# A third accumulator bank for the last part of a weight table, and two vector-engine steps in another order

## The reference, cut to what matters

```
x (32,32,512) f32
y0  = grouped_conv(x) + context + bias
out = oct_linear(silu(oct_linear(y0, Wgate)) * oct_linear(y0, Wup), Wdown)
x   = x + out                          # 1024 tokens of 512 values
y   = mix of 8 small kernels, by an attention net on cond_128, applied to x
x   = x + moe(y)                       # 32 experts, top 2, 512x512 each
```

## Time and profile before

| what | value |
|---|---|
| device time, median of 3 runs | 279.16 us (278.95 to 281.38) |
| the profiled execution: its own time | 279.04 us |
| its span, first to last instruction | 277.2 us |
| PE busy | 265.2 us, 96% of the span |
| DVE, ACT, POOL busy | 143.1, 77.8, 68.5 us |
| mean granted PE clock | 0.997 |

### The profile page before, as it was taken

How to read it: one execution, slowest core, us unless ns; L and a number is a source line. 1 busy time by engine, 2 the same in 40 slices (tenths; PEclk the granted TensorE clock), 3 DMA queues, 4 the chain that set the end, 5 groups by cost and what they waited for, 6 DMA issues and landing times.

```text
span 277.2 us, 4491 instructions
## 1 busy us (share of the span) xinstructions
PE 265.2 (96%) x1588; PEld 158.2 (57%) x1588; DVE 143.1 (52%) x423; ACT 77.8 (28%) x144; POOL 68.5 (25%) x67
## 2 busy tenths in 40 slices
PE   7888999999999999999999999999999999997991
PEld 3356677678866677878887665433333433332680
DVE  2577766766913342477541336520558521440885
ACT  1755564334212214233321121311011111113100
POOL 0711600000000000003705022453776352143200
PEclk9999999999999999999999999999999999999998
DMA  7999900000011100009905999962799999996937
GB/s 261 400 367 334 292 29 1 2 0 2 0 38 38 40 1 38 2 6 362 385 8 182 384 421 420 423 246 62 249 355 404 416 421 421 427 401 228 417 140 278
DMA packets 19590, 61.69 MB, mean 223 GB/s; under 512 B 4698, under 2 KB 6394, under 8 KB 15216
## 3 DMA queue, kind: packets, MB, share of 16 engines
q1 hardware_dynamic: 14816, 51.03, 47.7%
q0 software_dynamic: 3312, 7.80, 7.6%
q10 hardware_dynamic: 1440, 2.58, 2.5%
HBM read 54.39 MB, written 13.21 MB: 244 GB/s over the span
## 4 chain that ended last, share of the span: by engine, by line
PE 79%; DMA 8%; DVE 7%; issue 2%; SPq 1%; ACT 1%; DVEq 0%; ACTq 0%; POOLq 0%
PE bank L1452 29%; PE bank L1620 18%; PE bank L1655 15%; DMA wbuf<-r_tab 3%; PE bank L1507 3%; PE bank L1593 3%; DMA xp_first<-in_xp 3%; PE bank L1335 2%; DMA r_tab<-res,recs 2%; PE bank L1514 1%; PE bank L1345 1%; DVE acc L1308 1%; DVE acc L1303 1%; PE bank L1397 1%; PE bank L1564 1%
## 5 line engine op out<-in xcount | busy, mean ns | idle before, releaser
L1620 PE MATMUL bank<-wbuf,xT 128*32 128x512 f32 (+1 forms) x448 | 70.4, 597 | 1.8 <-DMA wbuf<-in_w 1.7
L1655 PE MATMUL bank<-md,hid 128*128 128x512 f32 x176 | 49.7, 418 | 0.0
L683 POOL DMA_INDIRECT slots<-kept,sid x16 | 15.9, 994 | 120.3 <-DVE sid L1072 117.3
L1620 PEld LDWEIGHTS bank<-wbuf,xT 128*32 128x32 f32 (+1 forms) x448 | 18.8, 119 | 37.6 <-issue 36.3
L1655 PEld LDWEIGHTS bank<-md,hid 128*128 128x128 f32 x176 | 31.3, 188 | 9.0 <-issue 4.1
L1452 PE MATMUL bank<-y0hi,mg 128*128 128x512 f32 x88 | 35.2, 412 | 0.2 <-ACT y0hi L758 0.2
L1452 PE MATMUL bank<-y0hi,mu 128*128 128x512 f32 x88 | 33.7, 396 | 0.7 <-DVE mu L958 0.7
L1452 PE MATMUL bank<-y0lo,mu 128*128 128x512 f32 x88 | 33.6, 393 | 0.0
L1452 PE MATMUL bank<-y0lo,mg 128*128 128x512 f32 x88 | 33.5, 392 | 0.0
L1109 DVE COPY xT<-bank 128x512 f32<-128x512 f32 x19 | 13.0, 690 | 37.6 <-PE bank L1593 36.0
L880 ACT ACTIVATE res<-bank,recs 128x512 f32<-128x512 f32 x19 | 13.1, 687 | 66.7 <-PE bank L1620 61.1
(11 more groups left out here) (208 smaller groups left out, 300.6 us busy)
## 6 DMA issues: line engine op xcount, KB each, us to landing
wbuf<-in_w SPq DMA_DIRECT2D x32, 1024.0 KB, 13.4
r_tab<-in_zero SPq DMA_DIRECT2D x1, 4096.0 KB, 25.8
wbuf<-r_tab SPq DMA_DIRECT2D x8, 512.0 KB, 7.3
acc<-in_x SPq DMA_DIRECT2D x1, 2048.0 KB, 15.2
y_tab<-yv SPq DMA_DIRECT2D x8, 256.0 KB, 5.1
out<-acc ACTq DMA_DIRECT2D x8, 256.0 KB, 2.4
base<-in_base SPq DMA_DIRECT2D x3, 352.0 KB, 7.2
xp_first<-in_xp SPq DMA_DIRECT2D x1, 1040.0 KB, 7.0
```

What stands on the lines that cost most here:

```text
L683: pool.indirect_dma_start(out=slots, out_offset=bass.IndirectOffsetOnAxis(ap=sid[:, j, k:k + 1], axis=0), in_=rec[:, j, k], in_offset=None ...
L1620: v = mm(RS[t % 2][p0:p0 + w], xT[x_slot(t)][:, c, p0:p0 + w], wbuf[buffer(r)][:, c], start=(c == 0), stop=(c == DC - 1))
L1655: v = mm(DN[j % 2][:], hid[:, t, part, c], md[:, c], start=(c == 0 and part == 0), stop=(c == HC - 1 and part == 1))
```

## The change

Up part 7 is made in bank 4 instead of bank 3. It waits for the first low half (`y0lo_done` at 1), the last reader of bank 4, in place of the copy of part 5, and it comes right behind part 5 on PE, ahead of part 6. The four gate products of chunk 1 are cut in two pairs with part 6 between them. `pu_mm` is counted in the new order. On DVE the copy of part 7 moves ahead of `conv_lo(1)`. In chunk 1 of the first half DVE does the copy of `up_rest(2)` first and `hid_lo(0)` behind it; all other chunks keep their order.

```diff
+UP_ORDER = (0, 1, 2, 3, 4, 5, 7, 6)
...
+        def up_bank(k):
+
+            return bank[4] if k == OCT - 1 else PU[k % 2]
...
             def up_table(k):
-                act.wait_ge(pu_mm, k + 1)
+                act.wait_ge(pu_mm, UP_ORDER.index(k) + 1)
...
             def up_table(k):
-                dve.wait_ge(pu_mm, k + 1)
-                nc.vector.tensor_copy(mu[:, :, 0:CUT, OB * k:OB * (k + 1)], in_bank(PU[k % 2], 0, CUT)).then_inc((pu_even, pu_odd)[k % 2], 1)
+                dve.wait_ge(pu_mm, UP_ORDER.index(k) + 1)
+                nc.vector.tensor_copy(mu[:, :, 0:CUT, OB * k:OB * (k + 1)], in_bank(up_bank(k), 0, CUT)).then_inc((pu_even, pu_odd)[k % 2], 1)
...
             conv_lo(0)
             up_table(5)
+            up_table(7)
             conv_lo(1)
-            up_table(7)
             conv_lo(2)
             conv_lo(3)
...
-                        if c >= 1:
+                        if c >= 2:
                             hid_lo(n - 1)
                         for kind, k in first:
                             if kind == "up":
                                 up_rest(k)
                             if kind == "down":
                                 down_high(k)
+                        if c == 1:
+                            hid_lo(n - 1)
                         hidden(n)
...
-                if k >= 2:
+                if 2 <= k < OCT - 1:
                     pe.wait_ge((pu_even, pu_odd)[k % 2], k // 2)
-                mm(in_bank(PU[k % 2], 0, CUT), perm[:, k], chunks(0, CUT)(tern[:, 1]), start=True, stop=True).then_inc(pu_mm, 1)
+                if k == OCT - 1:
+                    pe.wait_ge(y0lo_done, 1)
+                mm(in_bank(up_bank(k), 0, CUT), perm[:, k], chunks(0, CUT)(tern[:, 1]), start=True, stop=True).then_inc(pu_mm, 1)
...
-            def products(bank_, tab, n, half, parts):
-                for r in range(R):
+            def products(bank_, tab, n, half, parts, rs=range(R)):
+                for r in rs:
...
                 up_table(4)
                 up_table(5)
-                products(G[1], mg, 1, 0, (0,))
+                up_table(7)
+                products(G[1], mg, 1, 0, (0,), range(R // 2))
                 up_table(6)
-                up_table(7)
+                products(G[1], mg, 1, 0, (0,), range(R // 2, R))
                 pe.wait_ge(pu_even, OCT // 2)
                 pe.wait_ge(pu_odd, OCT // 2)
```

## The result

The changed kernel takes 278.09 us in the median of 10 runs (277.84 to 278.83), the kernel before 279.10 in 10 runs beside it (278.82 to 281.47). The ratio is 0.9956, with a 95% interval of 0.9936 to 0.9976; the two medians alone give 0.9964. The profiled execution after has a time of 278.11 and a span of 276.3, where before it was 279.04 and 277.2.

The account below looks back on a forecast made before the run. PE's order of work was taken to bound the kernel nearly everywhere. Gains of 0.48 and 0.32 make 0.80, so 279.04 - 0.80 = 278.24, stated as 278.3 given the runs' median, with a range of 277.7 to 279.3.

Parts of the forecast that it names:

- The first edit: PE, chunk 1: part 7 in bank 4 and part 6 between product pairs start the up products 0.48 us earlier.
- the hand-over: Copy to PE: 0.13 us from a copy's end to PE's start, used for every hand-over to PE.
- The second edit: DVE, chunk 1: up_rest(2) copied first opens PE's 0.69 stall; 0.32 comes through, 0.37 becomes a wait for POOL.
- rival (a): Down table: POOL is done in time or its hand-over is shorter, so all 1.17 comes, 277.9; chance 0.10.
- Rival (b): DVE and POOL: the moved low half meets POOL's L673, 0.80 shrinks to 0.11, 278.9; chance 0.07.
- To the end: From 32.5 to 245 us the chain stays on PE and the weight stream follows PE, so all 0.80 comes through.
- the wait for the last weights: Last stage: PE's 1.7 us wait before the last product, expected to stay near 1.7.
- Rival (c): Gain lost: up products no earlier, or weight stream doesn't follow PE and the last wait grows; 279.0, chance 0.14.
- Rival (d): Last stage: scatters or a load get ahead of the last weights on full DMA engines; 279.5, chance 0.11.

Follow-up runs that it names:

- e5: Changed kernel with the two waits ahead of the up products in the other order; one execution, 281.15 us, beside one of the kernel before of 281.61.
- e1: Only the part 7 and part 6 reordering, on the kernel before; DVE does hid_lo(0) first again in chunk 1; 282.98 us, ratio 0.9998.
- e6: e3 with part 6 in bank 7 and conv_lo(1) ahead of the copies of parts 5 and 7; one execution, 285.21 us, kernel before 281.61.
- e2: Only the DVE reordering in chunk 1 (copy of up_rest(2) ahead of hid_lo(0)), on the kernel before; ratio 0.9941.
- e3: Changed kernel with each part of the down table one place later on PE, ACT and DVE; 282.94 us, ratio 0.9962.
- e7: Kernel before with only the DVE reordering in chunk 1 and the down table one place later; one execution, 283.99 us, kernel before 281.61.
- r_before: The kernel before, unchanged, run and profiled once more on another chip than those with stops near 195 us; 279.13 us.

## Why the prediction was right

The forecast was 278.3 for a range of 277.7 to 279.3, and the median is 278.09. Against the profiled execution the sum said 0.80 less; that execution has 0.93 less, 1.12 when both are counted from the first gate product, and the medians differ by 1.01.

**The first edit.** Part 6 was forecast at 20.57 - 18.58 = 1.99 and came at 1.97, ACT's copy at 2.36 and came at 2.34, and ACT's copy is the last one. The up products were forecast at 3.03 and came at 2.88, the low products at 23.53 - 18.58 = 4.95 and came at 4.84. The term that was too large is the hand-over: I took 0.13 from the one row that had it and 0.05 for a start of the pipeline. Here it is 0.05 in all, and e5 shows that 0.1 of it goes with the order of the two waits. So the first edit is worth 0.63 at the up products, 0.59 at the low products and 0.57 further on (e1), instead of 0.48. I had the end of the first pair and the wait for the copy of part 4 as equal (20.56 and 20.57). In e6, without that wait, part 6 starts at the same place (1.98 against 1.97), so PE's own order is enough to set it.

**The second edit.** The stall of 0.69 opened up in full (0.14 between the rest parts), 0.31 of it came through, and 0.38 turned into the wait at L1407, where I had 0.32 and 0.37. e2 shows the same without the first edit, e3 and e7 show that 0.35 to 0.37 come back when the down table is asked for later. This was the step on which forecast and rival (a) differed, and POOL's three steps had the same lengths in every run, 2.05, 2.05 and 1.54, within 0.01.

**Rival (b)** asked that the low half hold POOL. It didn't: it ended at 28.66 + 0.73 = 29.39, POOL's last step started at 30.14, 0.09 behind the one before. What I had not seen is that the low half itself became short, 0.73 against 1.19 (below). It gave DVE 0.46 for which little came back: `hidden(1)` starts only at 29.61, after 0.21 of idle for which the profile names no one.

**To the end.** The 0.89 at 13.02 is 0.90 at conv 2, and at the first product of the last stage 0.97 (151.86 against 152.83). The end is 257.50 against 258.62, 1.12 less. The extra of about 0.2 lies in the last stage, and not in the wait for the last weights, which shrank from 1.7 to 1.0 where I had it near 1.7. The chain that ended last leaves PE for good at about 245 us, ten us before that wait ends: it goes on through an ACT copy, a scatter, SP and one load of the scattered rows, and then DVE to the end. In the kernel before (chain in order of time, 240 to 277 us):

```profile
245.18 0.70 ACT res L880
...
255.78 9.22 DMA wbuf<-r_tab
```

In the changed kernel, and in r_before:

```profile
255.05 8.99 DMA wbuf<-r_tab
```

```profile
256.11 8.96 DMA wbuf<-r_tab
```

The load starts 0.95 earlier (255.05 - 18.80 against 255.78 - 18.58) and is 0.23 shorter. It is as short in r_before, which is the kernel before, so the extra can't be put down to the edits. In r_before PE also starts its last product early, and its last sums at 239.26, where in the first profile it was 240.05, 0.79 earlier, but the end comes only 0.11 earlier (258.51 against 258.62). So a wait of 1.7 there doesn't set the end, and my reading that it would swallow the gain was wrong, as are the prices of rivals (c) and (d) as far as they hang on it; how long the wait could grow before it counts, no run shows. The forecast didn't suffer, because the wait is no term of its sum. Rival (c) falls with the first profile: the last product got its weights at 234.88, where before it was 236.48, so the stream moved with PE and more. Rival (d), a collision in the last stage, was not seen in the result's runs. The stops of the other chips show that a trouble in this stage is real and larger than I priced it, but what they showed was engines standing still, not loads in another order.

## What to carry to other kernels

A stall that is opened by moving a step only pays as far as the next late partner: work out from its own chain, here POOL's three steps, when it will be ready, and how far it moves with the first edit. Where the partner is late, ask later for what it makes; that was worth as much (0.37) as the part of the second edit that came through. Before you price a wait near the end, look where the chain that ended last leaves that engine: here the 1.7 before the last product lay behind it. And where a time can't resolve an edit, places counted from a common early instruction can, to 0.06; read more than one place, since a part of a gain at the first can be gone at the next (0.63 and 0.59) or come only there (0.11 and 0.22).

## What the runs showed of the hardware that I had not expected

**A low half on DVE beside POOL waits to a fixed point of POOL's step.** `hid_lo` takes 0.69 alone. Beside POOL's L671 (L677 after), which takes 2.05, it ended 0.69 after a point 0.71 behind POOL's start: 28.58 + 1.19 - 0.69 = 29.08 and POOL at 28.37; 30.78 + 1.19 - 0.69 = 31.28 and POOL at 30.57 (e1). In the changed kernel it starts 0.66 behind POOL's start, and takes only 0.73; in e2 0.67 behind, and takes 0.72. Beside L679, which takes 1.54, that point is 1.40 behind the start (31.00 + 1.23 - 0.69 = 31.54, POOL at 30.14; in the kernel before 31.46 + 1.13 - 0.69 = 31.90, POOL at 30.50). So it is held, but not to the end of POOL's row. The Trainium skill ("SBUF — State Buffer", Who interferes with whom) has a DVE instruction with two SBUF inputs contend with a POOL instruction that reads SBUF, and has the first one keep the shared ports for its whole instruction where the DVE instruction runs in a 2-port mode, which by the page a `tensor_tensor` like this one doesn't have. The traces agree with the contention; in them the hold ends 1.34 and 0.14 ahead of the end of POOL's row. Why, they don't tell. In the kernel before it made the low half 0.50 longer, so by estimate 0.50 of the 0.69 that PE stood at `up_rest(3)` was this contention; no run takes it away by itself.

**The order of two waits.** With the late semaphore in the first of two waits, PE started 0.05 behind the copy; with it in the second, 0.15 (e5), or 0.13 in the kernel before. At the low products 0.06 of that 0.1 is left (4.90 against 4.84). One pair of waits was tried.
